# First slots of a fused cross-attention and routed feed-forward kernel: the order of four input loads, of one zeroing and of one group of query matmuls

## The reference

```
def layer(x, ctx):
    q  = layernorm(x) @ Wq + bq
    k, v = split(ctx @ Wkv + bkv)
    p  = softmax(q k^T / 4)                    # per head, over the 128 keys
    x1 = x + (p v) @ Wo + bo
    n  = layernorm(x1)
    z  = gelu(n @ w_block)                     # for the 96 tokens with the largest n . w_router
    return x1 + where(selected, z, n)
```

## Time and profile before

| what | value |
|---|---|
| median of 3 runs | 903.54 us (903.44 to 903.98) |
| the profiled execution's own time | 904.1 us |
| its span in the trace | 902.3 us |
| PE, DVE, ACT, POOL busy, share of the span | 96%, 95%, 96%, 88% |
| ACT busy from 100 to 200 us | 99.70 of 100 us |
| mean granted TensorE clock | 0.991 |

### The profile page before, as it was taken

How to read it: one execution, slowest core, us unless ns; L and a number is a source line. 1 busy time by engine, 2 the same in 40 slices (tenths; PEclk the granted TensorE clock), 3 DMA queues, 4 the chain that set the end, 5 groups by cost and what they waited for, 6 DMA issues and landing times. The chain is left out here.

```text
span 902.3 us, 30174 instructions
## 1 busy us (share of the span) xinstructions
PE 864.8 (96%) x9842; PEld 718.8 (80%) x9842; DVE 857.9 (95%) x2068; ACT 870.6 (96%) x4632; POOL 789.6 (88%) x1489
## 2 busy tenths in 40 slices
PE   6999999999999999999999999999999999999972
PEld 6778888888888888888888888888888888888752
DVE  5888999999999999999999999999999999999987
ACT  4999999999999999999999999999999999999984
POOL 5468879999999999999999999999999999998865
PEclk9999999999999999999999999999999999999997
DMA  7221123232323232223333222323222323211102
GB/s 233 69 65 53 54 63 86 79 93 59 84 82 89 72 96 69 79 79 85 84 83 91 57 80 88 91 72 95 61 85 79 87 78 90 75 40 40 41 24 94
DMA packets 71357, 70.40 MB, mean 78 GB/s; under 512 B 12064, under 2 KB 63520, under 8 KB 71200
## 3 DMA queue, kind: packets, MB, share of 16 engines
q1 hardware_dynamic: 69840, 67.68, 26.4%
q10 hardware_dynamic: 1360, 0.79, 0.3%
HBM read 35.13 MB, written 16.78 MB: 58 GB/s over the span
## 5 line engine op out<-in xcount | busy, mean ns | idle before, releaser
L646 ACT ACTIVATE e_sb<-ps_s,neg_max 128x128 f32<-128x128 f32 x2048 | 772.1, 639 | 2.8 <-DVE neg_max L805 2.7
L646 ACT ACTIVATION_READ_ACCUMULATOR e_sb<-ps_s,neg_max 128x1 f32 x2048 | 718.2, 464 | 0.0
L805 DVE TENSOR_REDUCE neg_max<-ps_s 128x4 f32<-128x512 f32 x512 | 331.0, 666 | 19.7 <-PE ps_s L385 18.2
L385 PE MATMUL ps_s<-q_eo,k_sb 32*128 32x256 f32 x2048 | 146.6, 399 | 3.6 <-ACT e_sb L646 1.5
L450 PE MATMUL ps_a<-e_sb,v_pad 128*32 128x128 f32 x4096 | 138.4, 276 | 1.5 <-POOL v_pad L1168 0.9
L344 PE MATMUL ps_a<-w_o_sb,o_sb 128*128 128x256 f32 x512 | 131.7, 379 | 4.0 <-DVE v_sb L929 3.8
L450 PEld LDWEIGHTS ps_a<-e_sb,v_pad 128*32 128x32 f32 x4096 | 104.1, 109 | 23.2 <-issue 21.5
L385 PEld LDWEIGHTS ps_s<-q_eo,k_sb 32*128 32x128 f32 x2048 | 95.8, 184 | 32.9 <-issue 28.7
L344 PEld LDWEIGHTS ps_a<-w_o_sb,o_sb 128*128 128x128 f32 x512 | 93.8, 189 | 22.8 <-issue 4.7
L1157 POOL TENSOR_TENSOR x_sb<-x_sb,bo_sb 128x256 f32<-128x256 f32 x128 | 105.1, 822 | 0.2
L1168 POOL TENSOR_TENSOR v_pad<-v_sb,recip 128x256 f32<-128x256 f32 x128 | 79.5, 621 | 29.1 <-DVE recip L865 27.1
(11 more groups left out here) (113 smaller groups left out, 2213.8 us busy)
## 6 DMA issues: line engine op xcount, KB each, us to landing
x_sb<-in_x SPq DMA_DIRECT2D x64, 256.0 KB, 3.0
c_sb<-in_ctx SPq DMA_DIRECT2D x64, 256.0 KB, 3.0
out<-z_sb SPq DMA_DIRECT2D x64, 256.0 KB, 2.4
q_eo<-q_raw SPq DMA_DIRECT2D x504, 32.0 KB, 2.0
z_sb<-in_L_xattn_Wkv ACTq DMA_DIRECT2D x2, 256.0 KB, 6.7
z_sb<-in_L_xattn_Wq ACTq DMA_DIRECT2D x1, 256.0 KB, 3.6
w_z_sb<-in_L_ffn_w_block SPq DMA_DIRECT2D x1, 256.0 KB, 8.0
w_o_sb<-in_L_xattn_Wo SPq DMA_DIRECT2D x1, 256.0 KB, 7.1
```

Source lines behind the costliest of these rows:

```text
L385: mm = nc.tensor.matmul(ps_s[:, bank(b, j), c, :, :], k_sb[rows, r2, c, h * T:(h + 1) * T], q_eo[rows, r2, :, c, h, :], start=True, stop=True)
L646: last = nc.scalar.activation(e_sb[:, b % 3, j, c, par, :], ps_s[:, bank(b, j), c, par, :], ACT.Exp, bias=neg_max[:, b % 4, h:h + 1], accu ...
L805: nc.vector.tensor_reduce(neg_max[:, b % 4, :].rearrange("p (c j q) -> p j c q", c=C, j=J)[:, j, :, :], ps_s[:, bank(b, j), :, :, :], AX.X ...
```

## The change

Three places of the prologue are written in another order; no instruction is added or taken away on PE, DVE, ACT or POOL, and SP has the same DMAs.

```
@@ SP
             load_c(6)
             load_x(10)
             load_x(12)
+            queries_even_odd_of_pair(2)
+            load_c(8)
             load_x(14)
-            load_c(8)
             load_c(10)
-            queries_even_odd_of_pair(2)
+            queries_even_odd_of_pair(4)
             load_c(12)
+            load_x(16)
             load_c(14)
-            queries_even_odd_of_pair(4)
-            load_x(16)
             queries_even_odd_of_pair(6)
@@ PE, slots 2 and up
                 if s < 4:
                     transpose_inputs(2 * s + 5)
-                if s == 2:
-                    queries_or_keys_of_pair(6, 0)
...
                 attention(s - 1, sure)
+                if s == 2:
+                    queries_or_keys_of_pair(6, 0)
@@ POOL
             nc.gpsimd.memset(q_eo[:, 0, :, :, 2:4, :], 0.0).then_inc(q_eo_zero, 1)
-            nc.gpsimd.memset(q_eo[:, 1, :, :, :, :], 0.0).then_inc(q_eo_zero, 1)
...
             input_and_bias(0)
             input_and_bias(1)
+            nc.gpsimd.memset(q_eo[:, 1, :, :, :, :], 0.0).then_inc(q_eo_zero, 1)
             rstd1_of_pair(6)
```

## The result

The changed kernel takes 905.34 us in the median of 20 runs (903.98 to 907.42), the kernel before 903.70 us in the median of 20 (903.26 to 907.24). The ratio of the runs is 1.0015, with a 95% interval of 1.0008 to 1.0022: 1.4 us slower, 0.7 to 2.0.

The account below looks back on a forecast made before the run. ACT's work past the prologue was taken as the bound. Queries 1.2, zeroing 0 and loads 0 sum to +1.2 us on the median of 903.54, giving 904.7 us; range 903.5 to 906.0.

Parts of the forecast that it names:

- The bound: ACT past the prologue: busy 99.70 of 100 us, so a delay of its early start moves everything behind it.
- Queries behind the attention, +1.21 us: PE, end of slot 2: late queries delay DVE's copy and reciprocal, so scores of batch 3 start at 41.60, not 40.39.
- The zeroing, 0: POOL: zeroing moved to 15.97, ending about 17.8 in idle time until 25.01; cost 0, gain 0.
- the rival's exact pair: DVE's key copy of pair 0 at 16.45 beside POOL's zeroing; upper bound 1.3 us if DVE stood back.
- The loads, 0: SP's queue: stripes start no earlier; ctx 8, issued at 26.95, lands about 3 us before batch 8's transposes; cost 0.
- A swallowed delay: Rival at slot 3's scores: PE's order alone starts them where they were, or the delay is offset; about 903.6 us, chance 0.15.
- Ctx 8 too late: Rival at PE's transposes of batch 8 (33.51): a landing of 8.7 us costs 2.1 us; 906.9 us, chance 0.05.
- a blocked DVE: Rival: POOL's zeroing blocks DVE's key copy, scores of batch 0 wait; 1.3 + 1.2 = 2.5 us, 906.0 us, chance 0.05.
- Really faster: Rival: below 901.7 us; ACT must lose 1.8 us idle, its two gaps in slots 2 and 3 hold 1.56; chance 0.04.

Follow-up runs that it names:

- the PE edit alone: Kernel before with only the queries of pair 6 moved behind the attention of batch 1 on PE: 905.28 us against 903.96, ratio 1.0012 (1.0004 to 1.0021).
- their own run: Kernel before with only SP's new order of loads and stripes: 904.43 us against 903.87, ratio 1.0003 (0.9992 to 1.0014).
- one line moved on POOL: Kernel before with xhat of batches 9 and 11 made ahead of the scaled values: 903.01 us against 903.87; on another chip 901.32 against 902.09.

## Why the prediction was right

*The bound.* ACT's work past the prologue sets the end, so a delay in slot 3 is kept to the end. It held: the PE edit alone costs 9.07 - 7.86 = 1.21 us in slot 2 of the profile and 1.1 us (0.4 to 1.9) at the end.

*Queries behind the attention, +1.21 us.* Held step by step. With the zero at batch 9's transposes, attention +0.31 us (forecast 0.32), queries another 1.01 (1.03), DVE's copy another 39.03 - 37.25 = 1.78 (1.76), reciprocal another 0.60 (0.60), scores 39.89 - 39.63 = 0.26 behind its start (0.26). PE's idle time was forecast at about a microsecond and is 0.95, DVE's at 1.4 and is 1.37, ACT's gap at 1.2 and is 1.12.

*The zeroing, 0.* Held. Its place shifted: 17.13 instead of 16.0. Most of that is the xhat of batches 4 and 5 ahead of it, which started 0.89 us later (14.38 instead of 13.49), as POOL had waited 1.59 us for their statistics instead of 0.40; another 0.30 us were a wait for the output bias:

```profile
15.78 1.42 POOL L1156 TENSOR_TENSOR x_sb<-x_sb,bo_sb 128x256 f32<-128x256 f32 x2 [0.30 <-DMA bo_sb<-in_L_xattn_bo]
17.13 1.81 POOL L1260 MEMSET q_eo<- 128x2048 f32 x1
23.29 0.19 POOL L1135 TENSOR_SCALAR ve<-st 128x2 f32<-128x2 f32 x1 [4.35 <-DVE st L851]
```

POOL still waits 4.35 us behind it, less than the 7 us left by the earlier trace rows, but enough. In the run with the zeroing alone, `t_lo` (one input in PSUM, one in SBUF) took 0.69 us beside it, the same as in the profile after, where it had ended before the zeroing began. The Trainium skill's exception for DVE instructions with at most one SBUF input ("SBUF — State Buffer", section "Who interferes with whom") agrees with that. The key copy itself had ended before the zeroing began, so the rival's exact pair was not met; no DVE instruction with two SBUF inputs stood beside the zeroing.

*The loads, 0.* Held, both in the interval of their own run and in the order of SP's queue:

```profile
20.00 5.19 SPq L268 DMA_DIRECT2D q_eo<-q_raw  x8
25.24 0.58 SPq L247 DMA_DIRECT2D c_sb<-in_ctx  x1
25.86 0.47 SPq L239 DMA_DIRECT2D x_sb<-in_x  x1
```
```profile
31.81 0.44 PE L414 MATMUL ps_t<-ident,xhat 128*128 128x128 f32 x2
```

ctx 8 is issued at 25.24 and wanted at 31.81, 6.57 us later; by the rows of the kernel before, the end of the stripes of pair 2 (26.95) and the transposes of batch 8 (33.51) are 6.56 apart. The two ctx loads issued there took 3.0 and 3.6 us to land, which leaves about 3 us to spare, as forecast. PE does not wait there.

*One test that I set was failed.* I wrote that the prediction is wrong if anything ahead of 37 us moves by more than a few tenths. It moved by 1.7 us, to earlier. The step that failed there is a tacit one: that one profiled execution stands for the kernel. The profile before was an execution with half clock from 11.7 to 15.2 us, and that made 1.5 of the 1.7 us: from batch 2's transposes to the scores of batch 0 are 17.29 - 11.32 = 5.97 us in it and 15.56 - 11.13 = 4.43 in the profile after. The other 0.2 us is the start of these transposes. The net of 1.3 us in the two spans agrees with the forecast by chance. It is -1.7 (start of slot 1), +1.2 (slot 2), +1.1 and +0.5 (slot length up to copy 112), and +0.2 behind: only the +1.2 is the change.

*The total.* 904.7 was forecast from a median of 903.54; 905.34 came, 0.6 above. On both sides of the comparison the medians depend on which executions fall in; the ratio's +1.4 (0.7 to 2.0) holds the 1.2. What share of the executions has the longer slots or a half clock in either kernel can't be read from 20 runs without profiles, and stays open.

*The rivals.* A swallowed delay: no, the wait ahead of the scores is there in every profile in which the queries are late and their copy stands ahead of the reciprocal. Ctx 8 too late and a blocked DVE: no. Really faster: not by this change. But my reason for it was too narrow, and misread the rows. ACT has a third gap in slot 2, ahead of the copy of batch 8, in the profile before:

```profile
34.21 0.59 ACT L657 CAST t_hi<-ps_t 128x512 fp32r<-128x512 f32 x1 [0.41 <-PE ps_t L414]
```

With it the gaps hold 1.97 us, more than the 1.8 that I named as needed, and not 1.56. And I counted them as if nothing could reach them, where one line moved on POOL took 0.96 of it.

## What to carry to other kernels

When work is moved on one engine, look at who consumes it on the next engine, and at what stands right behind that consumer in its order: here the moved matmuls were wanted late, but their copy stood ahead of a small reciprocal for which the first engine waited. Look at whether a producer waits ahead of another operand that is ready: POOL stood waiting for the scaled values for 1.33 and 4.17 us, with an xhat behind them that it could have made meanwhile. And before a difference of a microsecond between two traces is explained, take a second trace of the same kernel: compare stretches between the same two instructions, not times from the start.

## What the runs showed of the hardware

- Executions of one program differ by stretches, in steps. The length of a slot is 6.686 us (six of 14 profiles) or 6.697 us (eight), from copy 3 to copy 105, in both kernels: 1.1 us over 102 slots. The seven slots behind take 47.05 to 47.07 us with the short ones and 47.53 to 47.56 with the long ones, but for one profile with xhat ahead of the scaled values (long slots, and 47.13). The longer slot is seen in ACT's exponentials: from 100 to 700 us the median from the start of one to the start of its accumulator read is 250 ns in the profiles with long slots and 249 in the others. Why an execution has one or the other is open.
- Early half clock: in 2 of 14 profiles TensorE was at 1.2 GHz for 3.4 us from 11.7 or 12.4 us on, and the scores of batch 0 started at 17.2 to 17.3 instead of 14.5 to 15.6. The clock's part of that is 1.5 us: from batch 2's transposes to these scores are 5.94 to 5.97 us in the two, and 4.43 to 4.47 in the twelve others. The rest is how late the transposes start. The two are also those in which PE had been idle longest ahead of these transposes (2.16 and 1.97 us); in the twelve with full clock it was 0.62 to 1.87 us, the longest with xhat ahead of the scaled values. No run sets this idle time by itself, so it is not shown to be the cause. Both profiles have the loads in their old place, but six others with the old place have full clock, so no link with the loads is shown.
- Late half clock: in 2 other profiles of the 14 TensorE was at 1.2 GHz for 3.4 us from 876.1 or 876.5 us on, and 98.0 us lie between copies 112 and 127 instead of 96.4 to 96.7. Ahead of it PE had been idle for 1.28 us in both, but the first profile of the kernel before has the same 1.28 us of idle time in that place (until 876.71) and full clock behind it: the same idle time goes with either level.
- In the first 80 us of the changed kernel the 256 KB loads of ctx took from 2.9 to 10.1 us to land. The two issued between 25 and 27 us, behind five us with a DMA share of 0.19, took 3.0 and 3.6 us.
